# Fillers and score masks on 128 rows, values that stream three to five copies, and a newly written order, in a two-layer attention, expert and top-k block

## The reference

```python
x = x + xattn0(layernorm(x), ctx, ctx, mask, ...)   # 16 heads of 8, softmax over the 77 keys
x = x + ffn0(layernorm(x), ...)    # attention among the 4 sequences, norm, 8 experts (gate by argmax, capacity 256), norm
x = x + xattn1(layernorm(x), ctx, ctx, Wq, Wk)      # 16 heads, only the 32 largest of 77 scores kept
x = x + ffn1(layernorm(x), ...)    # token shift, sigmoid(r) * (relu(k)**2 @ Wv)

# in xattn1
top_vals = jax.lax.top_k(scores, 32)[0]
masked = jnp.where(scores >= top_vals[..., -1:], scores, -jnp.inf)
e = jnp.einsum('bhqk,bhka->bhqa', softmax(masked), v)
```

## Time and profile before

| | us |
|---|---|
| median of 3 runs | 580.47 |
| lowest and highest | 578.23, 587.06 |
| the profiled execution | 588.05 |
| its span, first to last instruction | 586.2 |
| TensorE, products | 505.3 |
| VectorE | 482.3 |
| ScalarE | 290.8 |
| GpSimd | 278.9 |
| mean granted clock of TensorE, share of full | 0.819 |

### The profile page before, as it was taken

The page is one execution under the profiler, slowest core; times in us unless marked ns, Lnnn a source line. Parts: engine busy times, 40 slices in busy tenths (PEclk is TensorE's granted clock), DMA queues, the critical chain, the costliest instruction groups (busy, mean ns, idle before and its releaser), DMA issues.

```text
span 586.2 us, 11489 instructions
## 1 busy us (share of the span) xinstructions
PE 505.3 (86%) x2929; PEld 374.3 (64%) x2929; DVE 482.3 (82%) x3014; ACT 290.8 (50%) x797; POOL 278.9 (48%) x400
## 2 busy tenths in 40 slices
PE   5989997797996998699988898899889878798887
...
GB/s 293 246 0 1 2 1 1 1 1 1 2 1 1 1 2 1 0 2 1 2 6 5 2 5 2 7 7 1 7 6 5 2 7 6 2 11 6 1 6 9
DMA packets 5935, 9.64 MB, mean 16 GB/s; under 512 B 744, under 2 KB 4976, under 8 KB 5616
## 3 DMA queue, kind: packets, MB, share of 16 engines
...
q10 hardware_dynamic: 288, 0.56, 0.3%
...
## 4 chain that ended last, share of the span: by engine, by line
PE 43%; DVE 38%; ACT 7%; issue 6%; POOL 4%; DMA 1%; SPq 0%; DVEq 0%; ACTq 0%; POOLq 0%
DVE area_b L956 15%; DVE top L948 14%; PE psT L1320 8%; PE psM L1091 5%; PE psM L1288 3%; PE psM L1228 2%; PE psM L1236 2%; PE psS L1059 2%; PE psM L1034 2%; PE psT L1080 2%; PE psS L1062 2%; PE psM L1129 2%; PE psM L1223 1%; PE psM L1164 1%; DVE mx L715 1%
## 5 line engine op out<-in xcount | busy, mean ns | idle before, releaser
L1320 PE MATMUL psT<-mrow,mones 65*128 65x308 bf16 x608 | 118.2, 347 | 2.0 <-ACT vv L671 1.2
L948 DVE MAX8 top<-area_b 128x8 f32<-128x77 f32 x768 | 112.7, 226 | 0.0
L956 DVE MATCH_REPLACE8 area_b<-top,area_b 128x77 f32<-128x77 f32 x512 | 107.0, 226 | 0.0
L1320 PEld LDWEIGHTS psT<-mrow,mones 65*128 65x128 bf16 x608 | 68.5, 114 | 40.7 <-issue 14.1
L1091 PE MATMUL psM<-vblk,pT 128*128 128x81 f32 (+1 forms) x320 | 48.9, 319 | 9.4 <-ACT early L568 4.5
L1091 PEld LDWEIGHTS psM<-vblk,pT 128*128 128x128 f32 (+1 forms) x320 | 47.0, 234 | 12.8 <-issue 11.1
L956 DVE MATCH_REPLACE8 area_b<-top,area_a 128x77 f32<-128x77 f32 x256 | 53.6, 225 | 0.0
L1272 PE MATMUL psT<-consts,p 128*128 128x128 f32 (+1 forms) x160 | 35.4, 351 | 12.9 <-POOL p L433 8.2
L587 ACT ACTIVATE mparts<-psM,cur 128x128 f32<-128x128 f32 x128 | 38.0, 367 | 16.4 <-PE psM L1228 16.1
L1288 PEld LDWEIGHTS psM<-vblk,pT 128*128 128x128 f32 (+1 forms) x320 | 42.0, 212 | 6.4 <-issue 5.7
L1288 PE MATMUL psM<-vblk,pT 128*128 128x81 f32 (+1 forms) x320 | 43.5, 295 | 2.3 <-ACT pT L641 1.9
...
## 6 DMA issues: line engine op xcount, KB each, us to landing
...
area_b<-in_w SPq DMA_DIRECT2D x1, 2048.0 KB, 17.0
...
```

The source lines that it names most:

```text
L948: ins = e.max(tops[:, r, h], (left if r else scores_sb[t % RING])[:, h])
L956: ins = e.match_replace(left[:, h], tops[:, r, h], (left if r else scores_sb[t % RING])[:, h], GONE)
L1320: mm(bank[:, 0:B * KEYS], mones[:], mrow.rearrange("p b k -> p (b k)"), start=True, stop=True)
```

## The change

1. `mrow` and `mones` get 128 rows in place of 65. The fillers (L1331 now) and the mask terms of the first scores read 128 rows; the added rows are zero in `mrow` and one in `mones`.
2. The value products stream a number of copies that depends on the chunk: 3, 3, 4, 4 and then six times 5, as many as the bank holds behind the chunk's first column, in place of 3 always. Ten chunks stream 44 blocks of 27 columns in place of 30.
3. ORDER is another table. It has the same steps, other than fillers, in an order that is moved by up to some 35 places. It has 157 pairs of fillers in place of 304, the last of them beside top-k tile 5, and ten pairs named `stoke` in the last tile, which write the last scores bank and wait each for one of the last top-k steps.

```diff
-COPIES = 3
-FILLS = 304
-STOKES = 0
+FILLS = 157
+STOKES = 10
+BANK = 512
+
+
+def copies(c):
+    at = FIRST[c] * VE
+    return next((n, (BANK - at) // n) for n in (5, 4, 3) if (BANK - at) // n >= VW - at)
...
-        mrow = sb("mrow", [65, B, KEYS], BF16)
-        mones = sb("mones", [65, P], BF16)
+        mrow = sb("mrow", [P, B, KEYS], BF16)
+        mones = sb("mones", [P, P], BF16)
...
-        pvs0, pvs1 = (bank[:, 0:COPIES * VW].rearrange("p (r n) -> p r n", n=VW) for bank in (psM0, psM1))
-        pv0, pv1 = (v[:, 0].rearrange("p (h n) -> p h n", n=VE) for v in (pvs0, pvs1))
+        pv0, pv1 = (bank[:, 0:VW].rearrange("p (h n) -> p h n", n=VE) for bank in (psM0, psM1))
+
+        def streams(bank, c):
+            n, step = copies(c)
+            at = FIRST[c] * VE
+            return bank[:, at:at + n * step].rearrange("p (r n) -> p r n", n=step)[:, :, 0:VB]
...
-                            ins = mm(psS[:, g, 0:GW], mones[:], mrow[:, b, None, :].broadcast_to([65, HG, KEYS]), start=False, stop=True)
+                            ins = mm(psS[:, g, 0:GW], mones[:], mrow[:, b, None, :].broadcast_to([P, HG, KEYS]), start=False, stop=True)
...
-                            ins = mm(pvs1[:, :, FIRST[c] * VE:FIRST[c] * VE + VB], pT1[0:w, c],
-                                     vblk1[0:w, t // NJ, c, None, :].broadcast_to([w, COPIES, VB]), start=(c == 0),
+                            ins = mm(streams(psM1, c), pT1[0:w, c],
+                                     vblk1[0:w, t // NJ, c, None, :].broadcast_to([w, copies(c)[0], VB]), start=(c == 0),
```

The product with the values of the first attention changes in the same way. Of ORDER the lines at its end, before and now:

```diff
-value1@15 acts@14 half@14 value2@15 down@14 norm@15 fvalue@14 close@15 end@14 root@15 closen@15 fill@298 fill@299 fill@300 fill@301
-fill@302 fill@303 fturn@15 shift@15 up@15 acts@15 half@15 down@15 end@15""".split()
+fvalue@13 mark20@15 end@13 mark21@15 mark22@15 mark23@15 max30@15 max31@15 part0@15 part1@15 norm@14 stoke@157 stoke@158 stoke@159
+stoke@160 stoke@161 stoke@162 stoke@163 stoke@164 turn0@15 max32@15 add3@14 copy0@15 max33@15 sum4@14 part2@15 stoke@165 value0@15
+square4@14 part3@15 scale4@14 turn1@15 norm4@14 copy1@15 stoke@166 fturn@14 shift@14 turn2@15 value1@15 copy2@15 value2@15 up@14
+norm@15 close@15 acts@14 root@15 down@14 fvalue@14 half@14 closen@15 end@14 fturn@15 shift@15 up@15 acts@15 half@15 down@15 end@15""".split()
```

More of the change, by code:

```diff
@@ L1090, in value @@
                             w = P if c < NCH - 1 else LAST
[L1091 to L1092 removed]
+                            ins = mm(streams(psM0, c), pT[0:w, c],
+                                     vblk0[0:w, b, c, None, :].broadcast_to([w, copies(c)[0], VB]), start=(c == 0),
                                      stop=(c == NCH - 1), skip_group_check=True)
@@ L1344 @@
[L1344 to L1351, removed]
@@ L1408 @@
-half@4 max23@6 down@4 copy1@5 affine@8 turn@9 mark20@6 fvalue@4 turn2@5 copy@9 mark21@6 sum3@8 end@4 fill@150 moe0@9 square3@8
-mark22@6 copy2@5 scale3@8 value@5 mark23@6 gated0@9 max30@6 norm3@8 max31@6 max32@6 max33@6 moe1@9 max00@7 cut@6 max01@7 lturn@8
-lT@8 max02@7 gated1@9 fill@151 ask@8 norm@5 max03@7 qT@8 add3@5 fill@152 moe2@9 sign@6 scores@8 mark00@7 dif@7 mark01@7 mark02@7
-gated2@9 keep@8 keys@9 mark03@7 fill@153 fill@154 fill@155 fill@156 total@9 product@6 max10@7 sum4@5 max11@7 square4@5 max12@7
@@ L1416 @@
-fvalue@5 max03@8 norm@6 dif@8 sign@7 mark00@8 mark01@8 scores@9 mark02@8 add3@6 sum2@10 product@7 sum4@6 mark03@8 square2@10
-square4@6 max10@8 keep@9 max11@8 max12@8 max13@8 scale4@6 exp@8 fill@161 fill@162 fill@163 fill@164 fill@165 fill@166 fill@167
-fill@168 turn0@7 mark10@8 load@11 norm4@6 scale2@10 mark11@8 copy0@7 fill@169 fill@170 fill@171 fturn@6 shift@6 mark12@8 turn1@7
-keys@10 norm2@10 end@5 up@6 mark13@8 copy1@7 affine@10 max20@8 turn@11 acts@6 turn2@7 max21@8 copy@11 half@6 down@6 max22@8 sum3@10
@@ new lines @@
+scale2@3 max20@2 turn1@1 acts@0 max21@2 half@0 down@0 norm2@3 max22@2 copy1@1 affine@3 turn@4 copy@4 max23@2 turn2@1 mark20@2 sum3@3
+moe0@4 copy2@1 mark21@2 square3@3 fvalue@0 value@1 scale3@3 gated0@4 mark22@2 end@0 mark23@2 norm3@3 max30@2 max31@2 lturn@3 moe1@4
+lT@3 norm@1 max32@2 add3@1 ask@3 gated1@4 max33@2 cut@2 qT@3 fill@125 fill@126 moe2@4 sum4@1 scores@3 square4@1 gated2@4 total@4
+keep@3 scale4@1 sign@2 max00@3 keys@4 max01@3 max02@3 load@5 max03@3 sum2@4 mark00@3 square2@4 dif@3 norm4@1 mark01@3 fill@127
@@ new lines @@
+max30@3 gated2@5 scores@4 add3@2 max31@3 sum4@2 total@5 max32@3 square4@2 keys@5 keep@4 max33@3 scale4@2 max00@4 cut@3 norm4@2
+max01@4 fturn@2 shift@2 max02@4 sum2@5 up@2 max03@4 square2@5 load@6 sign@3 mark00@4 scale2@5 mark01@4 dif@4 mark02@4 norm2@5
+mark03@4 acts@2 turn@6 max10@4 product@3 down@2 copy@6 max11@4 fvalue@2 moe0@6 max12@4 max13@4 gated0@6 mark10@4 affine@5 fill@139
+fill@140 fill@141 turn0@3 exp@4 mark11@4 moe1@6 half@2 mark12@4 sum3@5 end@2 square3@5 mark13@4 copy0@3 scale3@5 gated1@6 fill@142
@@ new lines @@
+affine@9 mark13@7 turn@10 copy1@6 fturn@5 copy@10 turn2@6 max20@7 sum3@9 moe0@10 square3@9 max21@7 shift@5 max22@7 scale3@9
+gated0@10 up@5 max23@7 mark20@7 norm3@9 moe1@10 copy2@6 mark21@7 acts@5 lturn@9 half@5 mark22@7 value@6 gated1@10 mark23@7 lT@9
+max30@7 max31@7 moe2@10 max32@7 ask@9 gated2@10 down@5 max33@7 qT@9 total@10 fvalue@5 max00@8 cut@7 max01@8 max02@8 max03@8 mark00@8
+scores@9 dif@8 sign@7 norm@6 mark01@8 mark02@8 add3@6 sum2@10 product@7 square2@10 mark03@8 sum4@6 square4@6 max10@8 keep@9 max11@8
```

212 lines of the change are left out of this document (102 added, 110 removed).

## The result

| us | before | after |
|---|---|---|
| median of 4 runs each | 583.42 | 552.66 |
| lowest and highest | 578.23, 587.06 | 550.93, 555.6 |
| the profiled execution, its span | 588.05, 586.2 | 555.6, 553.8 |
| mean granted clock | 0.819 | 0.88 |

The changed kernel takes 0.9477 of the time, interval 0.9428 to 0.9526: 5.2% faster, against a forecast of 567 us. Its median lies 1.3 us under the low end of the stated range, 554, and beside rival (a), which gave 553.

The account below looks back on a forecast made before the run. It took VectorE to be the bound from 350 to 562 us, and TensorE, late at a low clock, before and behind. Sum: 588.05 - 13 - 6 + 2 + 0 - 4 = 567.05, so 567 us; range 554 to 581.

Parts of the forecast that it names:

- rival (a): Before 350 us: the clock hardly ever stays low, and VectorE's idle time goes nearly whole; 553 us, chance 0.12.
- term 2: Stretch 30 to 240 us: wider value products and 128-row masks end low-clock stretches somewhat sooner; -6 us, bounds 0 and -18.8.
- term 1: Stretch 240 to 350 us: 128-row fillers bring the clock back, VectorE idles less; -13 us, bounds 0 and -20.5.
- term 3: Cost of wider value streams and 13 more filler pairs before the last group's gates: +2 us, 0 to +16.
- The signs that it named for a right forecast: Before 350: no 0.50 stretch over some 15 us, clock above 0.85; VectorE idle 78.8 to about 60 before saturation.
- Term 4: Stretch 350 to 562 us, without fillers behind top-k tile 5: VectorE idles only 1.1 us, so 0 change.
- Rival (c): 366 to 506 us: without fillers the clock falls and TensorE becomes the bound; 600 us, at half 584; chance 0.10.
- Term 5: Tail: fillers ahead of the last turn go, tile 14's mixing products move behind the last values; -4 us.
- Rival (b): Whole kernel: rows do not matter to the clock; 587 us by the profiled execution, 579.5 for the runs; chance 0.16.

## Why the prediction was wrong in size

It named the mechanism rightly and failed in sizes, in the second term above all. Up to tile 5 it gave 17 us (terms 1 to 3) and 31.9 came: 9.1 of the difference are term 2's, 3.8 term 1's, and 2 the cost of term 3, which was not seen. From tile 15 on it gave 4 and none came (-0.2). With the 0.7 us between them that is the 11.4 between 567.05 and the 555.6 of the profiled execution. That it kept the sum absolute did no harm: the medians lie 30.8 us apart, the profiled executions 32.4. The stated range was said to take in rival (a), 553, and began at 554.

**What bounds the kernel; right.** The signs that it named for a right forecast came: before 350 us no stretch at 0.50 is longer than 10.2 us, the mean clock is 0.94, and VectorE's idle time from 30 us to tile 5's start fell from 78.8 to 48 us (320 us less 272.03 busy in 30 to 350 after), where the forecast wanted about 60.

**Term 1, stretch 240 to 350, -13.** The first instruction of tile 1's top-k (244.9 before, 229.8 after) stands almost at the border of the two stretches. From it to tile 5's (349.3, 317.4) it is 104.4 us before and 87.6 after: -16.8, near the bound of -20.5. The mechanism was as told: fillers at 138 in place of 257 ns and the three waits of the earlier trace rows nearly gone. "Two thirds" left 7.5 us of VectorE's idle time for a fall at the begin and for hand-overs; 4.2 stayed, and there was no fall (1.00 from 226 to 284). One ground in the prediction was thinner than it says: the 41 us at 0.50 hold products on 128 rows too, among them a value block, and the clock did not rise behind them. That the height of the fillers decides is shown by the runs, not by that row.

```profile
272.25 4.19 PE psM L1288 x20
```

**Term 2, stretch 30 to 240, -6: the step that failed, by size.** Up to tile 1 it gave 244.9 - 229.8 = 15.1 us, where the forecast took 6, a third of the 18.8 that VectorE idles inside four low stretches. It was wrong in two ways. "Somewhat sooner" was much sooner: the four stretches of the earlier trace rows, 54.8 us with 18.8 of VectorE idle, have four in their place in the changed kernel that add up to 23.9 us with 7.4 idle (the sum of four windows, columns as above):

```profile
sum 23.90, PE 20.77 PEld 15.13 DVE 16.52 ACT 7.00 POOL 9.34; mean PE 5.19 PEld 3.78 DVE 4.13 ACT 1.75 POOL 2.33
```

(93.1 to 96.5, 110.1 to 117.0, 130.6 to 134.0 and 171.6 to 181.8; in its second profiled execution the first and the third do not begin at all.) And the bound left out what lies outside those four. Three shorter stretches at 0.50, 35.7 to 42.5, 158.6 to 162.0 and 213.2 to 220.0, hold 7.5 us more of idle VectorE. The mean clock went from 0.83 to 0.93 in

```profile
30.00:228.00 198.00, 167.38 (x1137) 126.53 (x1138) 154.32 (x452) 79.29 (x187) 69.06 (x76) 0.93 0.00 1
```

that is from (1 - 0.83) / 0.5 x 210 = 71 us at the lower level to 0.07 / 0.5 x 198 = 28. The rows alone gave 12.0 us up to tile 1 (232.9), on 128-row fillers alone it was 8.8 (236.1), on copies alone 4.7 (240.2), and the whole change without any filler gave as much as with them (229.1). So the forecast looked rightly at real work here, and priced it too low. These are single executions, and the changed kernel's own second one has tile 1 at 225.1, so how the gain divides stays open.

Also VectorE pays for a low stretch behind it, not only in it. Term 1 was priced by all idle time of its stretch, and came near; in 243.9 to 291.7 itself VectorE idles 6.5 us (47.80 less 41.34), and 5.5 in the 10.3 us behind it at 1.00. Term 2 was priced by the idle time inside alone.

**Term 3, +2; near nothing.** A value step that streams 44 blocks of columns takes 2.48 to 2.59 us at the upper level, one of 30 took 2.36 to 2.43: 0.12 us a step, as worked out (at 0.50 it is 4.61 to 4.75 for 4.39 to 4.53). Before 350 there are 20 value steps and not 16, which changes nothing. No run shows the rest of the +2, the added fillers: the lengths hold it within what terms 1 and 2 gained.

**Term 4, 0; right.** Tile 5 to tile 15 took 195.6 us and 194.9. The changed kernel spent much more of it at 0.50, and in the longest such stretch it costs nothing: VectorE works 27.27 of 27.30 us.

```profile
472.00:499.30 27.30, 20.23 (x83) 16.58 (x83) 27.27 (x228) 13.50 (x37) 16.38 (x22) 0.50 0.02 6
```

Rival (c) fell there too: TensorE was busy 102.93 of 140 us at a clock of 0.76 in 366 to 506, above the 0.62 from which it would decide.

```profile
366.00:506.00 140.00, 102.93 (x545) 79.44 (x546) 139.13 (x1164) 95.70 (x277) 90.19 (x134) 0.76 0.02 5
```

**Term 5, -4: wrong, 0.** Its own step came: from the last top-k instruction to the end it is 15.7 us for 19.1, 3.4 less (forecast 3.0 at the lower clock), and the turn (L1314) starts at 547.79, 0.05 us behind the normalised tile. What failed is a step that it did not take: it looked at what was moved behind the last values, and not at what was put ahead of the cut on GpSimd. From tile 15's start to the last top-k instruction it is 25.8 us for 22.3, and the 3.5 are the new wait for tile 14's values. The second profiled execution lost 1.1 there (a wait of 1.43).

**Rival (a), chance 0.12, 553: nearest, partly by luck.** Up to tile 5 it is what happened: "both idle terms nearly whole", 32 us less 2 of cost, against 31.9. But it had 5 us in the tail, which did not come, and it counted from a profiled execution 4.6 us over the median of before; the profiled execution of the changed kernel took 555.6. The ground against it was that VectorE idles 11.5 of 40 us at 1.00 in 50 to 90, so latency holds much of the idle time. That is true of what stayed, 48 us; it said nothing of the idle time in and behind the low stretches, which was what the terms priced.

**Rival (b), 587.** It fell with the rows alone (556.6) and with the fillers of zeros on 128 rows (560.55). The trace had already spoken against the rule in the form of the Trainium skill, "TensorE: Matmul & The Clock Gate", section "What's actually happening" (the gate goes by how busy TensorE has been recently): 41 us busy at 0.50. The runs bear that out, with the number of rows as what it leaves out: the same instructions, as many and as wide, gave a mean clock of 0.81 to 0.87 at 65 rows (0.819 in the profiled execution), 0.897 at 96 and 0.932 at 128.
